# Routing decided from a centered image, product order on GpSimd, and a later routing step in a four-layer MetaFormer kernel

## The chip, the cores and the metric

The kernel runs on one core of a Trainium2 chip, as one launch. The core has five engines that run their own instruction streams in order and wait for each other by semaphores: TensorE (PE; PEld is its weight load), VectorE (DVE), ScalarE (ACT), GpSimd (POOL) and SyncE (SP, which here only issues DMAs). The metric is device microseconds of one execution. The kernel before took 395.4 us, the median of three runs (394.69, 395.40 and 400.83).

## The reference

Four layers act on x of 4 images with 128 channels and 16 x 16 pixels. Each layer adds a convolution-like block to x and then a mixture of experts (MoE), both behind a layer norm over the channels:

```python
x = x + _L0_conv_ref(_ln_c(x), ...)
t = _to_tokens(x)
t = t + _L0_ffn_ref(_ln_t(t), L0_ffn_gate_w, L0_ffn_experts)
...
x = x + _L3_conv_ref(_ln_c(x), L3_conv_conv_w, L3_conv_scale, L3_conv_wf)
t = t + _L3_ffn_ref(_ln_t(t), ...)
```

Layer 0's MoE routes by Sinkhorn and by a choice per expert and image:

```python
gates = jnp.einsum('bhnd,hde->bhne', x4, gate_w)
cg = sinkhorn(gf)                       # clip at 1e-10, 8 times: normalise over tokens, then over experts
vals, idx = jax.lax.top_k(jnp.transpose(cg, (0, 2, 1)), m)   # m = 32 tokens of each expert
gate_values = (vals > 0.5)
outputs = jnp.einsum('hmei,eio->hmeo', routed, experts) * gate_values
s = zeros.at[idx].add(outputs); c = zeros.at[idx].add(1.0)
out = s / (c + 1.0)
```

Layer 3's convolution block is a saliency map: `fm = relu(sal * w)`, `fm = where(fm > TH, fm, 0)`, `1 - wf * sigmoid(scale * fm)`. The MoEs of layers 1 to 3 take each token's two best of 8 experts; that of layer 3 has a hidden width of 256 where the others have 512.

## The kernel before

Channels lie on the 128 partitions and the 1024 pixels (4 images of 256; 8 tiles of 128 tokens) along the free axis. One block of code per engine holds that engine's instructions in program order, and named semaphores (`s["..."]`) order them; there is no scheduler, so the order written is the order run. `step` on DVE issues an instruction and waits for its end before the next one.

Layer 0 ends with an output convolution, image by image. Image 3 is last: DVE adds it to x, PE centers it (`late_center`, into PSUM bank 7), ACT squares it, PE forms the variance of its 256 pixels on all partitions (`late_variance`, L582), ACT takes Ln and Exp (L994, L996), DVE multiplies (L1332), PE forms the gates of tiles 6 and 7 (`gate_tiles`, L586), and DVE clips all gates into `plan`. `keep_clock` issues matmuls on zeros ("quiet", L463) that compute nothing. Then come eight Sinkhorn rounds: PE sums `plan` over tokens (L632) and computes two of the sixteen expert products (`expert_rows`, L625 to L627) while DVE runs six small steps; ACT copies each product out of PSUM (L1043).

After the rounds DVE forms `gate` (plan > 0.5) and `share` = gate / max(1, number of gates of the token) (L1356 to L1359). Tokens' expert outputs are multiplied by their gates: tiles 0 to 4 by ACT (40 ACTIVATEs, L1049) and summed by PE (L650, L651), tiles 5 to 7 by GpSimd (L384) which also sums them (L387, L389). Meanwhile DVE finds each expert's 32 best tokens per row in four rounds of MAX and MATCH_REPLACE (L1364, L1365); PE turns the result (L647), and DVE makes from it a factor per token (`picks`: L1372 to L1378) that scales the sums (L1381 to L1385).

Layers 1 to 3 run six MoE blocks, two halves of x in each layer: 48 units of one expert on 512 columns (block kb = 0 to 5, unit n = 8 kb + j). PE interleaves `front(n+1, f)` (first product) with `back(n, f)` (second product), as `first_half` and `second_half`; each product is three matmuls L440, L441, L442. ACT evaluates each hidden chunk twice (`hidden`, L1082 and L1083), DVE forms the low part (`low`, L1449) that `back` waits for, and `scale` (L1459) weighs a unit's result with its scores; GpSimd adds it to x (`add_part`, L408). While block 4 runs on the one half of x, block 5's half goes through layer 3's convolution block, its norm and its routing: `threshold` (L1588), `saliency_half` (L1593), `center(7, 1)` (L447), `variance(7, 1)` (L452), `logits(5)` (L749), `route_start`, `route_pick` (L1490 to L1502), `route_exp(5)` on ACT (L1088), `route_end` (L1525 to L1533), `turn_route(5)` on PE (L760), `keep_rows(5)` (L1546); SP then writes the scores' rows out and reads them back spread over all partitions (L299, L308). Where each of these stands among the units is written out as (j, f) in the loops.

Of the kernel before, what the change touches and what calls it, by code (L numbers as in the profile page):

```python
# [20 lines left out]
C = 128  # L21
# [42 lines left out]
for _name, _cols in [("center", C), ("mean", C), ("eps6", 1), ("eps5", 1), ("ident", C), ("ones", C),  # L64
# [32 lines left out]
    "gates_done", "expert_out", "expert_kept", "sink_in", "sink_sum", "plan_turned", "plan_ready",  # L97
    "gate_ready", "gated", "gated_sum", "pool_gated", "pool_sum",
# [12 lines left out]
def metaformer(nc, dram, out):  # L111
    ctx = ExitStack()
    with ctx:
# [40 lines left out]
        picked = bot[0:E, :]  # L154

# [35 lines left out]
        pick_w, cnt = piece(64), piece(8)  # L191
# [4 lines left out]
        half_wf, rest_wf, half_b, half_scale = [piece(1) for _ in range(4)]  # L196
        gate, share = oh1, oh2
# [151 lines left out]
        def _(pool):  # L349
# [31 lines left out]
            pool.wait_ge(s["gate_ready"], 1)  # L381
            for t in range(POOL_T, TT):
                tile = wb[:, t, :].rearrange("p (e c) -> p e c", c=C)
                pool.tensor_tensor(tile, tile, over(gate[:, t * E:(t + 1) * E], C), ALU.mult).then_inc(s["pool_gated"], 1)  # L384
# [53 lines left out]
        def _(pe):  # L438
# [141 lines left out]
            def late_variance():  # L580
                pe.wait_ge(s["squared"], 4)
                pe.matmul(bank(0, cols=PIX), k("mean"), image(sq, 3), start=True, stop=True).then_inc(s["variance"], 1)  # L582
# [6 lines left out]
            def early_gates():  # L589
                pe.wait_ge(s["early_normed"], 1)  # L590
                gate_tiles((4, 5))
# [11 lines left out]
            keep_clock(2, 5)  # L603
            late_variance()
            keep_clock(5, 5)
            pe.wait_ge(s["normed"], 4)
            gate_tiles((6, 7)).then_inc(s["gates_done"], 1)
# [325 lines left out]
            for j in range(E):  # L933
# [4 lines left out]
                elif j == 4:  # L938
                    variance(7, 1)
                elif j == 5:  # L940
                    logits(5)
                elif j == 7:
                    turn_route(5)
# [3 lines left out]
                elif j == 2:  # L947
                    saliency(1)
                elif j == 3:
                    center(7, 1)  # L950

# [7 lines left out]
        def _(act):  # L959
# [15 lines left out]
            def norm(n, split=None):  # L975
# [3 lines left out]
                if n == 1:  # L979
# [12 lines left out]
                    act.activation(image(sq, 3), bank(7, cols=PIX), ACT.Square).then_inc(s["squared"], 1)  # L992
                    act.wait_ge(s["variance"], 4)
                    act.activation(image(rstd, 3), bank(0, cols=PIX), ACT.Ln, bias=k("eps5")).then_inc(s["log_var"], 1)  # L994
# [190 lines left out]
            for j in range(0, E + 1):  # L1185
                for f in range(2):
# [18 lines left out]
                    elif (j, f) == (6, 1):  # L1205
# [7 lines left out]
        def _(dve):  # L1213
            steps = [0]

            def step(ins):

                steps[0] += 1
# [112 lines left out]
            dve.wait_ge(s["rstd"], 4)  # L1331
            dve.tensor_tensor(image(xn, 3), bank(7, cols=PIX), image(rstd, 3), ALU.mult).then_inc(s["normed"], 1)  # L1332

            dve.wait_ge(s["gates_done"], 1)
            dve.tensor_scalar(plan, bank(4, cols=64), 1e-10, None, ALU.max).then_inc(s["sink_in"], 1)
            plan3 = tiles(plan)
            for it in range(8):
# [8 lines left out]
                if it == 0:  # L1348
                    dve.wait_ge(s["norm_hi"], 4)
# [9 lines left out]
            step(dve.tensor_tensor(tiles(share), tiles(gate), over(r8b, E), ALU.mult))  # L1359
# [12 lines left out]
            step(dve.tensor_scalar(pick_w, bank(4, cols=64, first=64), 0.0, None, ALU.is_lt))  # L1372
            step(dve.tensor_reduce(cnt, tiles(pick_w), AX.X, ALU.add))
            step(dve.tensor_tensor(pick_w, pick_w, share, ALU.mult))
            step(dve.tensor_scalar(cnt, cnt, 1.0, None, ALU.add))
            step(dve.tensor_reduce(r8, tiles(pick_w), AX.X, ALU.add))
# [348 lines left out]
            for j in range(1, E + 1):  # L1725
                n = 4 * E + j
                for f in range(2):
# [21 lines left out]
                    elif (j, f) == (7, 0):  # L1749
                        route_end(5)  # L1750
                    elif (j, f) == (8, 0):
# [132 lines left out]
```

## Time and profile before

| | before |
|---|---|
| three runs | 394.69, 395.40, 400.83 us |
| the profiled execution | 396.52 us, with a span of 394.5 us from first to last instruction |
| busy: PE, ACT, DVE, POOL | 377.2, 289.7, 260.5, 156.0 us |
| mean granted clock of PE | 0.996 of full speed |
| up to Sinkhorn's first sum (L632) | 52.59 us |
| from there to the factor per token (L1381) | to 83.91 us |
| block 4 with the preparation of block 5 | about 323 to 369 us |

All times are from the start of the span of one profiled execution. A busy PE is not a PE at its peak, since matmuls overlap; what an engine waited for stands in brackets behind the instruction.

### The profile page before, as it was taken

The numbers are of one execution on the slowest core, as the hardware profiler recorded it, in microseconds if no ns is written. First come the engines' busy times: TensorE is split into PE (matmuls) and PEld (weight loads), VectorE is DVE, ScalarE is ACT, GpSimd is POOL, SyncE is SP. The second block draws the span as 40 slices with busy tenths as digits, with TensorE's granted clock in tenths as the row PEclk, the third lists the DMA queues.
The fourth block names the chain that finished last, engine by engine and source line by source line (L and its number), as shares of the span: only waits on it lengthen the run. The fifth ranks groups of instructions, "written<-read, shape, count | busy, mean of one in ns | idle before, by whom it ended". The sixth has DMA issues, their size and how long they took to land.

```text
span 394.5 us, 5148 instructions
## 1 busy us (share of the span) xinstructions
PE 377.2 (96%) x1664; PEld 274.8 (70%) x1668; DVE 260.5 (66%) x570; ACT 289.7 (73%) x515; POOL 156.0 (40%) x135
## 2 busy tenths in 40 slices
PE   8999989989999999999999999999999999989895
PEld 3688856445567687887877677877777777646784
DVE  0755656965434864785675986649957497676776
ACT  4552445935106778978889889999899998867883
POOL 5413000920298265123575781212133356332235
PEclk9999999999999999999999999999999999989999
DMA  7950000000000136604110031151120012220332
GB/s 252 446 197 1 2 0 0 2 0 0 2 0 0 32 135 212 265 2 133 28 53 0 2 109 28 45 200 49 41 95 28 27 27 82 55 80 1 90 99 82
DMA packets 11019, 28.64 MB, mean 73 GB/s; under 512 B 1246, under 2 KB 2526, under 8 KB 10736
## 3 DMA queue, kind: packets, MB, share of 16 engines
q1 hardware_dynamic: 10992, 28.31, 20.7%
q8 instruction: 13, 0.21, 0.2%
q14 instruction: 14, 0.11, 0.1%
HBM read 27.69 MB, written 0.62 MB: 72 GB/s over the span
## 4 chain that ended last, share of the span: by engine, by line
PE 67%; DVE 14%; ACT 14%; issue 3%; POOLq 0%; POOL 0%; DVEq 0%; ACTq 0%
PE ps L440 17%; PE ps L441 16%; PE ps L442 16%; ACT hidh L1082 4%; ACT ps L1083 4%; PE ps L447 4%; DVE hidl L1449 2%; PE ps L738 2%; PE ps L452 2%; ACT rstd L967 1%; DVE bot L1365 1%; ACT rstd L969 1%; PE ps L463 1%; DVE small L1364 1%; PE ps L541 1%
## 5 line engine op out<-in xcount | busy, mean ns | idle before, releaser
L1449 DVE TENSOR_TENSOR hidl<-ps,hidh 128x512 fp32r<-128x512 f32 x160 | 108.4, 687 | 53.7 <-ACT ps L1083 52.3
L408 POOL TENSOR_TENSOR x<-x,parts 128x512 f32<-128x512 f32 x43 | 55.9, 1301 | 149.2 <-DVE parts L1459 98.2
L440 PE MATMUL ps<-xh,wh_all 128*128 128x512 f32 x160 | 74.8, 468 | 2.2 <-DVE hidl L1449 1.7
L1082 ACT ACTIVATE hidh<-ps,par 128x512 fp32r<-128x512 f32 x96 | 68.1, 709 | 9.3 <-PE ps L442 7.6
L440 PE MATMUL ps<-hidh,wh_all 128*128 128x512 f32 (+1 forms) x162 | 64.5, 398 | 4.1 <-DVE hidl L1449 3.8
L1083 ACT ACTIVATE ps<-ps,par 128x512 f32<-128x512 f32 x96 | 65.4, 681 | 0.0
L441 PE MATMUL ps<-xh,wl_all 128*128 128x512 f32 x160 | 63.6, 397 | 0.0
L441 PE MATMUL ps<-hidh,wl_all 128*128 128x512 f32 (+1 forms) x162 | 63.6, 392 | 0.0
L442 PE MATMUL ps<-xl,wh_all 128*128 128x512 f32 x160 | 63.2, 395 | 0.0
L442 PE MATMUL ps<-hidl,wh_all 128*128 128x512 f32 (+1 forms) x162 | 63.1, 390 | 0.0
L398 POOL TENSOR_TENSOR wl_all<-wa,wh_all 128x512 fp32r<-128x512 f32 x40 | 51.3, 1299 | 3.5
L1082 ACT ACTIVATE hidh<-ps 128x512 fp32r<-128x512 f32 x64 | 38.3, 599 | 10.9 <-PE ps L442 10.8
L440 PEld LDWEIGHTS ps<-xh,wh_all 128*128 128x128 f32 x160 | 30.2, 189 | 18.5 <-DVE hidl L1449 7.7
L440 PEld LDWEIGHTS ps<-hidh,wh_all 128*128 128x128 f32 x162 | 30.5, 188 | 14.7 <-DVE hidl L1449 4.8
L1083 ACT ACTIVATE ps<-ps 128x512 f32<-128x512 f32 x64 | 38.4, 600 | 0.0
L441 PEld LDWEIGHTS ps<-xh,wl_all 128*128 128x128 f32 x160 | 30.3, 189 | 9.3 <-issue 4.6
L442 PEld LDWEIGHTS ps<-hidl,wh_all 128*128 128x128 f32 x162 | 30.5, 189 | 7.0
L441 PEld LDWEIGHTS ps<-hidh,wl_all 128*128 128x128 f32 x162 | 30.7, 189 | 6.6
L442 PEld LDWEIGHTS ps<-xl,wh_all 128*128 128x128 f32 x160 | 30.2, 189 | 7.2
L962 ACT ACTIVATE sq<-ps 128x512 f32<-128x512 f32 x15 | 9.2, 610 | 24.0 <-PE ps L447 24.0
L1236 DVE TENSOR_TENSOR xn<-ps,rstd 128x512 f32<-128x512 f32 x13 | 9.0, 692 | 25.3 <-ACT rstd L969 25.3
L1459 DVE SCALAR_TENSOR_TENSOR parts<-ps,par,scores_all 128x512 f32<-128x512 f32 x31 | 23.1, 745 | 2.1 <-PE ps L442 1.8
(254 smaller groups left out, 581.4 us busy)
## 6 DMA issues: line engine op xcount, KB each, us to landing
scores_all<-rows_scratch SPq DMA_DIRECT2D x48, 256.0 KB, 3.4
wa<-in_moe SPq DMA_DIRECT2D x2, 4096.0 KB, 15.6
wa<-in_moe SPq DMA_DIRECT2D x1, 2048.0 KB, 9.2
dft_o<-in_dft_o SPq DMA_DIRECT2D x1, 640.0 KB
w<-in_w_out SPq DMA_DIRECT2D x1, 576.0 KB, 7.8
cst<-in_consts SPq DMA_DIRECT2D x1, 512.5 KB, 6.8
x<-in_x SPq DMA_DIRECT2D x2, 256.0 KB, 3.1
we<-in_w_experts SPq DMA_DIRECT2D x1, 512.0 KB, 8.6
```

Of the source, the lines that this page charges most:

```text
L398: last = pool.tensor_tensor(wl_all[:, e, cols], wa[:, e, cols], f32(wh_all[:, e, cols]), ALU.subtract)
L408: pool.tensor_tensor(half(x, h), half(x, h), parts[:, n % 2, :], ALU.add).then_inc(s["state_added"], 1)
L440: pe.matmul(o, wh, xhi, start=start, stop=False)
L441: pe.matmul(o, wl, xhi, start=False, stop=False)
L442: return pe.matmul(o, wh, xlo, start=False, stop=stop)
L447: pe.matmul(bank(center_bank(n, h)), k("center"), half(x, h), start=True, stop=True).then_inc(s["centered"], 1)
L962: act.activation(work(sq, n, h), bank(center_bank(n, h)), ACT.Square).then_inc(s["squared"], 1)
L1082: act.activation(hidh[:, n % 2, f, :], sums, func, bias=bias).then_inc(s["hidden_hi_act"], 1)
L1083: act.activation(sums, sums, func, bias=bias).then_inc(s["hidden"], 1)
L1236: dve.tensor_tensor(half(xn, h), centered, work(rstd, n, h), ALU.mult).then_inc(s["normed"], 1)
L1449: dve.tensor_tensor(hidl[:, n % 2, f, :], bank(sums_bank(n, f)), f32(hidh[:, n % 2, f, :]), ALU.subtract).then_inc(s["hidden_lo"], 1)
L1459: dve.scalar_tensor_tensor(parts[:, n % 2, :], bank(part_bank(n)), p(spec["b2"])[:, e:e + 1], scores_all[:, slot, :], ALU.add, ALU.mult).t ...
```

## The change

Five edits.

- **Gates of the last image.** DVE copies the centered image out of PSUM (`late`, in the storage of `bot`). PE forms the gates of tiles 6 and 7 from that copy (`late_gates`, bank 3) and the variance of each token as one column per tile (`token_variance`, bank 2); ACT takes Ln and Exp of these two columns; DVE multiplies the gates by them while it clips them into `plan`. The clipping of the other six tiles stands ahead of that. The image's full variance, its Ln and Exp stay, behind this; its normed values are formed after the first round's steps and their low part after the second's. Three quiet matmuls stand where five stood.
- **GpSimd's products** wait for `share` too, and `share` is no longer a `step`.
- **Picks** take six steps where seven stood: the comparison with its 1/8 per expert (in place of the 1.0 that was added later), the comparison times `share` as one instruction, two sums, a reciprocal, a product.
- **`threshold`** compares the values in PSUM bank 7 in place of those in SBUF.
- **Block 5's routing** stands later: `logits(5)` and `turn_route(5)` behind their unit's second half, `route_exp(5)` behind (7, 1) in place of (6, 1), `route_end(5)` behind (7, 1) in place of (7, 0), `keep_rows(5)` behind (8, 1) in place of (8, 0).

```diff
@@ gpsimd
             pool.wait_ge(s["gate_ready"], 1)
+            pool.wait_ge(s["share_ready"], 1)
             for t in range(POOL_T, TT):
...
@@ tensor
             def late_variance():
-                pe.wait_ge(s["squared"], 4)
-                pe.matmul(bank(0, cols=PIX), k("mean"), image(sq, 3), start=True, stop=True).then_inc(s["variance"], 1)
+                pe.wait_ge(s["late_log"], 1)
+                pe.matmul(bank(2, cols=PIX), k("mean"), image(sq, 3), start=True, stop=True).then_inc(s["variance"], 1)
...
-                gate_tiles((4, 5))
+                gate_tiles((4, 5)).then_inc(s["most_gates"], 1)
+
+            def token_variance():
+                pe.wait_ge(s["squared"], 4)
+                for i in range(2):
+                    last = pe.matmul(bank(2, cols=1, first=i), sq[:, (6 + i) * C:(7 + i) * C], k("mean")[:, 0:1], start=True, stop=True)
+                last.then_inc(s["late_variance"], 1)
+
+            def late_gates():
+                pe.wait_ge(s["late_kept"], 1)
+                for i in range(2):
+                    last = pe.matmul(bank(3, cols=E, first=i * E), late[:, i * C:(i + 1) * C], p("gate_w"), start=True, stop=True)
+                last.then_inc(s["gates_done"], 1)
...
             keep_clock(2, 5)
+            token_variance()
+            late_gates()
             late_variance()
-            keep_clock(5, 5)
-            pe.wait_ge(s["normed"], 4)
-            gate_tiles((6, 7)).then_inc(s["gates_done"], 1)
+            keep_clock(3, 5)
...
-                elif j == 5:
-                    logits(5)
-                elif j == 7:
-                    turn_route(5)
                 second_half(4 * E + j)
...
+                elif j == 5:
+                    logits(5)
+                elif j == 7:
+                    turn_route(5)
@@ scalar
+                    act.wait_ge(s["late_variance"], 1)
+                    act.activation(late_rstd, bank(2, cols=2), ACT.Ln, bias=k("eps5")).then_inc(s["late_log"], 1)
+                    act.wait_ge(s["late_log"], 1)
+                    act.activation(late_rstd, late_rstd, ACT.Exp, scale=-0.5).then_inc(s["late_rstd"], 1)
                     act.wait_ge(s["variance"], 4)
...
-                    elif (j, f) == (6, 1):
+                    elif (j, f) == (7, 1):
                         route_exp(5)
@@ vector
-            dve.wait_ge(s["rstd"], 4)
-            dve.tensor_tensor(image(xn, 3), bank(7, cols=PIX), image(rstd, 3), ALU.mult).then_inc(s["normed"], 1)
+            dve.wait_ge(s["centered"], 4)
+            dve.wait_ge(s["squared"], 4)
+            dve.tensor_copy(late, bank(7, cols=PIX)).then_inc(s["late_kept"], 1)
+            dve.wait_ge(s["most_gates"], 1)
+            dve.tensor_scalar(plan[:, 0:6 * E], bank(4, cols=6 * E), 1e-10, None, ALU.max)
             dve.wait_ge(s["gates_done"], 1)
-            dve.tensor_scalar(plan, bank(4, cols=64), 1e-10, None, ALU.max).then_inc(s["sink_in"], 1)
+            dve.wait_ge(s["late_rstd"], 1)
+            for i in range(2):
+                last = dve.tensor_scalar(plan[:, (6 + i) * E:(7 + i) * E], bank(3, cols=E, first=i * E), late_rstd[:, i:i + 1], 1e-10,
+                                         ALU.mult, ALU.max)
+            last.then_inc(s["sink_in"], 1)
...
                 if it == 0:
+                    dve.wait_ge(s["rstd"], 4)
+                    dve.tensor_tensor(image(xn, 3), late, image(rstd, 3), ALU.mult).then_inc(s["normed"], 1)
+                elif it == 1:
...
-            step(dve.tensor_tensor(tiles(share), tiles(gate), over(r8b, E), ALU.mult))
+            dve.tensor_tensor(tiles(share), tiles(gate), over(r8b, E), ALU.mult).then_inc(s["share_ready"], 1)
...
-                dve.scalar_tensor_tensor(fm, fm, TH, fm, ALU.is_gt, ALU.mult).then_inc(s["sal_ready"], 1)
+                dve.scalar_tensor_tensor(fm, bank(7), TH, fm, ALU.is_gt, ALU.mult).then_inc(s["sal_ready"], 1)
```

PE between the last image's centering and the first Sinkhorn sum; `bot` holds the copy of the centered image, `par` the gate weights, `quiet` zeros. Before:

```order
166 L578 MATMUL ps<-x,cst 128x256 [waits x1_ready]
167 L586 MATMUL ps<-par,xn 128x8 [waits early_normed]
168 L586 MATMUL ps<-par,xn 128x8
169 L463 MATMUL ps<-quiet 128x512 x2
170 L582 MATMUL ps<-sq,cst 128x256 [waits squared]
171 L463 MATMUL ps<-quiet 128x512 x5
172 L586 MATMUL ps<-par,xn 128x8 [waits normed]
173 L586 MATMUL ps<-par,xn 128x8
174 L632 MATMUL ps<-small,cst 128x64 [waits we_split,sink_in,norm_lo,norm_hi]
```

Now:

```order
169 L466 MATMUL ps<-quiet 128x512 x2
170 L599 MATMUL ps<-cst,sq 128x1 [waits squared]
171 L599 MATMUL ps<-cst,sq 128x1
172 L605 MATMUL ps<-par,bot 128x8 [waits late_kept]
173 L605 MATMUL ps<-par,bot 128x8
174 L585 MATMUL ps<-sq,cst 128x256 [waits late_log]
175 L466 MATMUL ps<-quiet 128x512 x3
176 L647 MATMUL ps<-small,cst 128x64 [waits we_split,sink_in,norm_lo,norm_hi]
```

The gates no longer wait for `normed`; the full variance and three quiet matmuls now stand between them and the first sum.

DVE around block 5's routing, from the unit before it (`hidl` is `low`, `parts` is `scale`). Before:

```order
412 L1502 MATCH_REPLACE small<-small 128x8 [waits dve_step]
413 L1502 MATCH_REPLACE small<-small 128x8 x3
414 L1449 TENSOR_TENSOR hidl<-ps,hidh 128x512 [waits hidden,hidden_hi_act,dve_step]
415 L1525 SCALAR_TENSOR_TENSOR small<-small 128x32 [waits exp_out]
416 L1526 TENSOR_REDUCE small<-small 128x4 [waits dve_step]
417 L1532 RECIPROCAL small<-small 128x4 [waits dve_step]
418 L1533 TENSOR_TENSOR small<-small 128x32 [waits dve_step]
419 L1459 SCALAR_TENSOR_TENSOR parts<-ps,par,scores_all 128x512 [waits state_added,scores2_in,part_sums]
420 L1449 TENSOR_TENSOR hidl<-ps,hidh 128x512 [waits hidden,hidden_hi_act] x2
421 L1546 COPY rows<-ps 8x512 [waits rows_stored,route_turned]
422 L1459 SCALAR_TENSOR_TENSOR parts<-ps,par,scores_all 128x512 [waits state_added,scores3_in,part_sums]
```

Now:

```order
416 L1476 TENSOR_TENSOR hidl<-ps,hidh 128x512 [waits hidden,hidden_hi_act,dve_step]
417 L1486 SCALAR_TENSOR_TENSOR parts<-ps,par,scores_all 128x512 [waits state_added,scores2_in,part_sums]
418 L1476 TENSOR_TENSOR hidl<-ps,hidh 128x512 [waits hidden,hidden_hi_act]
419 L1552 SCALAR_TENSOR_TENSOR small<-small 128x32 [waits exp_out]
420 L1553 TENSOR_REDUCE small<-small 128x4 [waits dve_step]
421 L1559 RECIPROCAL small<-small 128x4 [waits dve_step]
422 L1560 TENSOR_TENSOR small<-small 128x32 [waits dve_step]
423 L1476 TENSOR_TENSOR hidl<-ps,hidh 128x512 [waits hidden,hidden_hi_act]
424 L1486 SCALAR_TENSOR_TENSOR parts<-ps,par,scores_all 128x512 [waits state_added,scores3_in,part_sums]
425 L1476 TENSOR_TENSOR hidl<-ps,hidh 128x512 [waits hidden,hidden_hi_act]
426 L1573 COPY rows<-ps 8x512 [waits rows_stored,route_turned]
```

The four steps of `route_end` moved from ahead of a unit's scaling to behind it, and the rows leave DVE one chunk later.

The picks on DVE. Before:

```order
111 L1372 TENSOR_SCALAR small<-ps 128x64 [waits picked_turned]
112 L1373 TENSOR_REDUCE small<-small 128x8 [waits dve_step]
113 L1374 TENSOR_TENSOR small<-small 128x64 [waits dve_step]
114 L1375 TENSOR_SCALAR small<-small 128x8 [waits dve_step]
115 L1376 TENSOR_REDUCE small<-small 128x8 [waits dve_step]
116 L1377 RECIPROCAL small<-small 128x8 [waits dve_step]
117 L1378 TENSOR_TENSOR small<-small 128x8 [waits dve_step]
```

Now:

```order
114 L1399 TENSOR_SCALAR small<-ps 128x64 [waits picked_turned]
115 L1401 SCALAR_TENSOR_TENSOR small<-ps,small 128x64 [waits share_ready]
116 L1402 TENSOR_REDUCE small<-small 128x8 [waits dve_step]
117 L1403 TENSOR_REDUCE small<-small 128x8
118 L1404 RECIPROCAL small<-small 128x8 [waits dve_step]
119 L1405 TENSOR_TENSOR small<-small 128x8 [waits dve_step]
```

One instruction fewer, and two that no longer wait for the one ahead of them.

## Rows read from the trace of the kernel before

**Rows 1.** The page: PE's granted clock in 40 slices (tenths).

```profile
PEclk9999999999999999999999999999999999989999
```

**Rows 2.** Chain of waits, last image to Sinkhorn: start us, us, engine and line.

```profile
48.87 0.34 PE ps L586 x4
...
49.66 0.45 PE ps L582 x2
...
51.56 0.63 PE ps L586 x4
...
52.59 0.42 PE ps L632 x2
...
54.57 0.45 PE ps L632 x2
```

**Rows 3.** Timeline: a small Ln on ACT, and quiet matmuls (idle before in brackets).

```profile
104.61 0.27 ACT L1069 ACTIVATE small<-ps,cst 128x4 f32<-128x4 f32 x1 [1.40 <-PE ps L707]
...
49.93 1.24 PE L463 MATMUL ps<-quiet 128*128 128x512 bf16 x5
```

**Rows 4.** Timeline from the shares to the factor per token.

```profile
69.20 11.80 ACT L1049 ACTIVATE wb<-wb,small 128x128 f32<-128x128 f32 x40
69.25 5.61 POOL L384 TENSOR_TENSOR wb<-wb,small 128x1024 f32<-128x1024 f32 x3 [35.38 <-ACT wb L1043]
...
69.58 1.65 DVE L1359 TENSOR_TENSOR small<-small 128x64 f32<-128x64 f32 x1
...
79.59 1.12 PE L650 MATMUL ps<-wb,cst 128*128 128x512 f32 x2
...
80.33 0.99 POOL L389 TENSOR_TENSOR sq<-wb 128x384 f32<-128x384 f32 x1
...
80.56 0.38 PE L651 MATMUL ps<-wb,cst 128*128 128x128 f32 x2
...
81.53 0.65 PE L647 MATMUL ps<-cst,bot 8*128 8x8 f32 x8 [0.59 <-DVE bot L1365]
...
83.91 0.69 DVE L1381 TENSOR_TENSOR sq<-ps,small 128x512 f32<-128x512 f32 x1
```

**Rows 5.** Timeline around layer 3's second threshold (L1588), in block 4.

```profile
344.81 1.28 POOL L408 TENSOR_TENSOR x<-x,parts 128x512 f32<-128x512 f32 x1 [5.58 <-DVE parts L1459]
...
345.27 0.69 DVE L1449 TENSOR_TENSOR hidl<-ps,hidh 128x512 fp32r<-128x512 f32 x1 [0.61 <-ACT ps L1083]
...
346.77 1.38 POOL L408 TENSOR_TENSOR x<-x,parts 128x512 f32<-128x512 f32 x1 [0.68 <-DVE parts L1459]
...
346.93 1.77 DVE L1588 SCALAR_TENSOR_TENSOR sq<-sq 128x512 f32<-128x512 f32 x1
...
349.36 0.50 PE L440 MATMUL ps<-hidh,wh_all 128*128 128x512 f32 x1 [1.61 <-DVE hidl L1449]
...
352.16 0.60 ACT L962 ACTIVATE sq<-ps 128x512 f32<-128x512 f32 x1 [0.42 <-PE ps L447]
...
353.50 0.69 ACT L1082 ACTIVATE hidh<-ps,par 128x512 fp32r<-128x512 f32 x1 [0.74 <-PE ps L442]
```

**Rows 6.** Busy time in a stretch: length, PE, PEld, DVE, ACT, POOL, clock, DMA, GB/s.

```profile
350.00:354.00 4.00, 4.00 (x9) 2.28 (x8) 2.19 (x4) 2.84 (x6) 1.27 (x1) 0.57 0.13 44
```

**Rows 7.** Timeline: block 4's routing (first row), then block 5's.

```profile
321.16 0.98 DVE L1525 SCALAR_TENSOR_TENSOR small<-small 128x32 f32<-128x32 f32 x1
...
363.62 0.23 ACT L1088 ACTIVATE small<-small 128x32 f32<-128x32 f32 x1 [2.27 <-DVE small L1494]
...
365.95 0.47 PE L440 MATMUL ps<-hidh,wh_all 128*128 128x512 f32 x1 [1.37 <-DVE hidl L1449]
...
370.50 14.62 SPq L308 DMA_DIRECT2D scores_all<-rows_scratch  x8
...
375.71 0.74 DVE L1459 SCALAR_TENSOR_TENSOR parts<-ps,par,scores_all 128x512 f32<-128x512 f32 x1
```

**Rows 8.** The page: DMA issues, with size and median us to landing.

```profile
scores_all<-rows_scratch SPq DMA_DIRECT2D x48, 256.0 KB, 3.4
```

More of the change, by code:

```diff
@@ L96 @@
     "out_conv_done", "x1_ready",
-    "gates_done", "expert_out", "expert_kept", "sink_in", "sink_sum", "plan_turned", "plan_ready",
-    "gate_ready", "gated", "gated_sum", "pool_gated", "pool_sum",
+    "most_gates", "gates_done", "late_kept", "late_variance", "late_log", "late_rstd", "expert_out", "expert_kept", "sink_in", "sink_sum", "plan_turned", "plan_ready",
+    "gate_ready", "share_ready", "gated", "gated_sum", "pool_gated", "pool_sum",
     "picked", "picked_turned", "combined", "combined_turned", "x2_ready",
@@ L154, in metaformer @@
         picked = bot[0:E, :]
+        late = bot[:, 0:PIX]
         with ExitStack() as scope:
@@ L190, in metaformer @@
         plan, r8, r8b, top8 = piece(64), piece(8), piece(8), piece(8, E)
-        pick_w, cnt = piece(64), piece(8)
+        pick_w, pick_s, cnt = piece(64), piece(64), piece(8)
         kmx, kbias, kes, krs = [piece(4, KK) for _ in range(4)]
@@ L196, in metaformer @@
         half_wf, rest_wf, half_b, half_scale = [piece(1) for _ in range(4)]
+        late_rstd = piece(2)
         gate, share = oh1, oh2
@@ L992, in norm @@
                     act.activation(image(sq, 3), bank(7, cols=PIX), ACT.Square).then_inc(s["squared"], 1)
+                    act.wait_ge(s["late_variance"], 1)
+                    act.activation(late_rstd, bank(2, cols=2), ACT.Ln, bias=k("eps5")).then_inc(s["late_log"], 1)
+                    act.wait_ge(s["late_log"], 1)
+                    act.activation(late_rstd, late_rstd, ACT.Exp, scale=-0.5).then_inc(s["late_rstd"], 1)
                     act.wait_ge(s["variance"], 4)
-                    act.activation(image(rstd, 3), bank(0, cols=PIX), ACT.Ln, bias=k("eps5")).then_inc(s["log_var"], 1)
+                    act.activation(image(rstd, 3), bank(2, cols=PIX), ACT.Ln, bias=k("eps5")).then_inc(s["log_var"], 1)
                     act.wait_ge(s["log_var"], 4)
@@ L1214, in _, with step @@
             steps = [0]
-            def step(ins):
-                steps[0] += 1
+            def step(ins, n=1):
+                steps[0] += n
                 ins.then_inc(s["dve_step"], 1)
@@ L1370, in _ @@
             dve.wait_ge(s["picked_turned"], 1)
[L1372 to L1376, printed above, removed]
+            marks = bank(4, cols=64, first=64)
+            dve.tensor_scalar(pick_w, marks, 0.0, 1.0 / E, ALU.is_lt, ALU.add).then_inc(s["dve_step"], 1)
+            dve.wait_ge(s["share_ready"], 1)
+            step(dve.scalar_tensor_tensor(pick_s, marks, 0.0, share, ALU.is_lt, ALU.mult), 2)
+            dve.tensor_reduce(cnt, tiles(pick_w), AX.X, ALU.add).then_inc(s["dve_step"], 1)
+            step(dve.tensor_reduce(r8, tiles(pick_s), AX.X, ALU.add), 2)
             step(dve.reciprocal(r8b, cnt))
@@ L1748, in _ @@
                         route_pick(5)
-                    elif (j, f) == (7, 0):
+                    elif (j, f) == (7, 1):
                         route_end(5)
-                    elif (j, f) == (8, 0):
+                    elif (j, f) == (8, 1):
                         keep_rows(5)
```

## The prediction

> **What bounds the kernel now.** I read the page first. PE is busy for nearly all of the span (the table above), and its granted clock is at full speed in all slices but one, the thirty-sixth [rows 1]. So most of the span is PE's own work, which the change leaves as it is; it can win only where PE waits for a decision, or runs at the lower clock. Three such places touch the edits.
>
> The first, in the chain of waits, is the last image's way to Sinkhorn: everything from its variance at 49.66 to the first sum at 52.59 hangs on one chain over PE, ACT, DVE and PE again [rows 2]. The rounds behind it repeat at 52.59, 54.57 and so on, 2.0 us each, and DVE's small steps and the sum set their pace, so whatever moves the first sum moves all of them.
>
> The second is the stretch from the shares to the factor per token [rows 4]. The last share instruction on DVE, a product of 128x64, shows 1.65 us, where seven later steps of that size take 1.73 together (82.18, L647's end, to 83.91). GpSimd's first product runs from 69.25 for 1.87 (5.61 for three), to 71.12; the share ends at 71.23. It stood behind GpSimd.
>
> The third is the second threshold in block 4: 1.77 us, while GpSimd's addition runs from 346.77 to 348.15 [rows 5]. PE then waits 1.61 us for the low part behind it, and from 350 to 354 the granted clock averages 0.57 [rows 6]: the lower of the two levels, 1.2 GHz, for most of it. No other slice has such a fall [rows 1]. Later in block 4 ACT waits 2.27 us for the routing and PE 1.37 us [rows 7].
>
> **Gates of the last image.** The old chain is variance, Ln, Exp, product, gates, clipping. The new one is shorter on ACT and DVE, but PE does its work in order, and I follow PE. It is free of quiet matmuls at 49.66. The token variances are four passes like those of L586, 0.34; the gates four more, 0.34. Then, still ahead of the first sum, come the full variance, 0.45 as before [rows 2], and three quiet matmuls, three fifths of 1.24 = 0.74 [rows 3]. The sum can start at 49.66 + 0.34 + 0.34 + 0.45 + 0.74 = 51.53. Is `plan` there by then? Ln of two columns is nearest to the 0.27 of four [rows 3]; with as much for Exp and twice 0.25 for the clipping it is ready at 50.0 + 0.27 + 0.27 + 0.5 = 51.0. So PE's queue ends last, and the gain is 52.59 - 51.53 = 1.06; I take **1.0**. Bounds: 0.5, if each group of four passes costs the 0.63 that L586 shows behind an idle PE [rows 2], to 1.5, if the variance and the quiet matmuls cost nothing. The copy of the centered image on DVE runs beside the token variances. The moved product and low part fall into the first and second round's wait for the sum on PE (0.45 each [rows 2]); if that cover failed, each would cost what it overruns. ACT copies expert products one round later, and has the rest of the rounds to catch up.
>
> **Shares and picks.** With GpSimd behind the shares, L1359 takes about 0.25: DVE's search starts 1.4 us sooner, and ends near 80.1 in place of 81.5. GpSimd starts some 0.65 later and ends at 81.32 + 0.65 = 81.97 [rows 4]; its sums are wanted behind L1381, so that is covered. But the 1.4 us do not all arrive. When the search ends, PE still has the seventh expert's pair to finish, until 80.94, so the turning starts there and ends at about 81.6. From there the steps took 1.73; one step fewer, and two that don't wait, leave about 1.3: 82.95. PE's last pair, behind the turning, takes 1.35 (79.59 to 80.94) and ends near 82.9 as well. ACT's forty products end at 81.0 either way. So L1381 starts near 83.0 and not at 83.91: **0.9**. Bounds: 0.4, if a step with two operands in SBUF meets GpSimd's last addition; 1.5, where ACT's end at 81.0 and PE's last 1.35 alone decide.
>
> **Threshold.** The low part L1449 at 345.27 reads one operand in PSUM and one in SBUF, and takes 0.69 though GpSimd's addition covers nearly all of it (344.81 to 346.09) [rows 5]. The threshold's new form reads the same way, so I price it at 0.74, as the scaled product L1459 of that form [rows 7]: 1.03 less. PE's wait of 1.61 then shrinks to 0.6. A wait of 1.37 us at 364.6 was followed by no fall of the clock [rows 1, 7], so I expect none here; at an average of 0.57 PE lost 4 x 0.43 = 1.7 us of work [rows 6]. PE would be 1.03 + 1.7 = 2.7 us ahead at the next variance. ACT can't follow all the way: besides the 1.03 it had only 0.42 and 0.74 of waiting for PE to give up there [rows 5], so what reaches the norm and the routing of block 5 is 1.03 + 0.42 + 0.74 = **2.2**. Bounds: 1.0, if the clock falls all the same; 2.7, if ACT is not the limit.
>
> The Trainium skill (SBUF — State Buffer, section "SBUF: two separate sides") states that DVE, with two SBUF inputs, and GpSimd take a shared pair of ports for a whole instruction, and that the later one blocks. The ends 71.23 behind 71.12 and 348.70 behind 348.15 agree with that [rows 4, 5]. By this rule the next edit loses on DVE; if DVE and GpSimd shared the ports without blocking, the sum would be 4.8 us in place of 4.1.
>
> **Block 5's routing later.** ACT no longer waits 2.27 us, and PE's wait for the low part behind the routing's picks shortens by the hidden chunk that ACT evaluates earlier, about half of 1.37: 0.7 won. But the moved end of the routing now comes behind a unit's scaling, which starts GpSimd's addition of some 1.3 us [rows 5]. In block 4's routing the same instruction, L1525, stands like that, and takes 0.98 [rows 7]. PE, which turns the result, waits that much longer: some 0.7 lost. I take **0**, with 0.7 either way. The rows leave DVE a chunk later in the program. Before, the reads of the scores were issued from 370.50, and the first one was used at 375.71 [rows 7], 5.2 us later; against the 3.4 that the page gives for landing [rows 8], that is 1.8 of slack. The units come 2.2 earlier and the rows only about 0.4, so the slack is just used up.
>
> **The sum.** 1.0 + 0.9 + 2.2 + 0 = 4.1 us. All three lie ahead of PE-bound work that follows at its own pace, so they should stay in the span: 394.5 becomes 390.4, and the profiled execution's 396.5 becomes 392.4. Its time stands 1.1 above the median of the runs, 395.4; on that scale the forecast is **391.3**.
>
> **Rivals.**
> - *The clock still falls in block 4*, there or at one of the shorter waits left behind it. For: the page shows that PE is one long wait from it. Against: a wait of 1.37 passed unharmed. Then the threshold is worth only 1.0, the sum 2.9: 392.5.
> - *The late rows starve the last block.* DVE would wait for the scores at its first scaling, with the low parts that PE needs queued behind it. For: the slack is used up, by the count above. Against: the low parts are a chunk ahead of PE there. With 1 to 2 us of waiting it costs as much at most: 392.3 to 393.3.
> - *Slower: the clock falls at Sinkhorn's start.* Two quiet matmuls are gone just where PE waits. At half speed a round is bound by PE: a sum of 0.45 [rows 2] and six product matmuls, which fill most of the round's 2.0 now, would take some 3.5, 1.5 more per round. Three slow rounds eat the gain; all eight cost 12, and the time would be 403. Against: in the new order PE has work from 49.66 to the sum with hardly a gap, and in the old order it stood idle behind its five quiet matmuls and kept the clock.
> - *No collision*, so that the late routing wins its 0.7 and the picks come at their bound: 5.4 in all, 390.0.
>
> **How the numbers follow.** The forecast gets 64 in 100, the clock in block 4 13, the late rows 9, the slower case 4, the better case 10. The terms' own bounds, not all at one end, reach from 2.0 to 5.8: 389.6 to 393.4. Some of the first two rivals' share, with the spread of about 1 us between runs that this kernel shows (394.69, 395.40), takes the upper end to 394.2. A change of 2%, about what a measurement of this kernel can tell from no change, is 7.9 us: faster by that needs nearly twice the sum, 0.04; slower by that needs nearly all eight rounds at half speed, 0.03; within it, 0.93.
>
> **What would show it.** The first Sinkhorn sum about 1.0 earlier, right behind the quiet matmuls; the last share at 0.25 and GpSimd's first product behind it; L1381 1.9 earlier by the clock of the span; both thresholds near 0.74, and no clock below full speed in any slice; ACT's 2.27 gone, and L1525's successor at about 1 us behind a scaling. I am wrong if the first sum waits for `plan`, or if PE's waits in block 4 come back elsewhere so that the last block starts less than 3 us earlier.

## The result, and the profile after

| | before | after |
|---|---|---|
| median, 22 runs each | 395.65 us | 393.94 us |
| the 22 runs | 394.45 to 400.85 | 392.16 to 397.08 |
| profiled execution | 396.52, span 394.5 | 392.55, span 390.6 |

The ratio, formed from fast runs alone (a run is slow when it lies over 1.5% above the fastest of its kernel), is 0.9949 [0.9929, 0.9969]: the change gained about 2 us by it and 1.7 by the medians, where 4.1 were forecast. The profiled execution alone did what was forecast, 396.52 to 392.55 against 392.4. So two things have to be explained: which terms of the sum are right in that execution, and why the median moved by less than half as much.

For after and for all later runs, the span and PE's mean granted clock of each run are on record. They are used to sort the runs, because the clock turned out to be the difference between them.

The page of after, with its span and the clock in 40 slices, stands against [rows 1]; the slice at 350 us is at full speed now:

```profile
span 390.6 us, 5157 instructions
...
PEclk9999999999999999999999999999999999999999
```

**A common point.** Two spans can't be laid over each other from their start. Up to 49 us both kernels run the same work, yet the low part of the third image on DVE, ahead of every edit, starts at different times. It is the first row of each fence; the second is DVE's reading of the first Sinkhorn sum. Timeline rows of before:

```profile
48.88 0.43 DVE L1330 TENSOR_TENSOR xl<-xn,xh 128x256 fp32r<-128x256 f32 x1 [0.48 <-ACT xh L990]
...
53.03 0.23 DVE L1342 TENSOR_REDUCE small<-ps 128x8 f32<-128x64 f32 x1 [0.59 <-PE ps L632]
```

and of after:

```profile
49.18 0.43 DVE L1349 TENSOR_TENSOR xl<-xn,xh 128x256 fp32r<-128x256 f32 x1 [0.48 <-ACT xh L1005]
...
52.20 0.23 DVE L1365 TENSOR_REDUCE small<-ps 128x8 f32<-128x64 f32 x1 [0.90 <-PE ps L647]
```

After comes 0.30 later here, and not by an edit: over the fourteen traces of this study this row lies between 47.77 and 49.18, in no order of the edits, and at 48.88 and 48.52 in two executions of the kernel before. From this row to the sum, before takes 4.15 us and after 3.02: the gates gained **1.13**. Read from the start of the span it would be 0.83. Every "shift" below is counted from this row.

PE's way to that sum in after, from the chain of waits (start us, us, engine and line); compare [rows 2]:

```profile
50.30 0.48 PE ps L605 x4
50.78 0.57 PE ps L585 x2
51.35 0.65 PE ps L466 x3
```

It is the order that the prediction followed: gates, full variance, three quiet matmuls, sum, with no wait for `plan`. (The chain leaves out the token variances, L599, which come ahead of these.)

The stretch from the shares to the factor per token in after (timeline); compare [rows 4]:

```profile
68.36 11.81 ACT L1068 ACTIVATE wb<-wb,small 128x128 f32<-128x128 f32 x40
...
68.75 0.23 DVE L1385 TENSOR_TENSOR small<-small 128x64 f32<-128x64 f32 x1
...
69.14 5.62 POOL L387 TENSOR_TENSOR wb<-wb,small 128x1024 f32<-128x1024 f32 x3 [34.99 <-DVE small L1385]
...
80.04 0.66 PE L662 MATMUL ps<-cst,bot 8*128 8x8 f32 x8
...
81.59 0.38 PE L666 MATMUL ps<-wb,cst 128*128 128x128 f32 x2
...
82.08 0.69 DVE L1408 TENSOR_TENSOR sq<-ps,small 128x512 f32<-128x512 f32 x1 [0.16 <-PE ps L666]
```

The share takes 0.23 in place of 1.65, and GpSimd starts behind it. The turning (L662) starts when PE ends the seventh pair, and what L1408 waits for last, by 0.16 us, is PE's last pair (L666): the bound that the prediction named. It starts at 82.08 against 83.91, a shift of -2.13, of which the gates are 1.13.

The threshold in block 4 in after, with PE's wait behind it, and block 5's routing (timeline); compare [rows 5, 7]:

```profile
345.02 1.40 POOL L411 TENSOR_TENSOR x<-x,parts 128x512 f32<-128x512 f32 x1 [0.68 <-DVE parts L1486]
...
345.19 0.68 DVE L1615 SCALAR_TENSOR_TENSOR sq<-ps,sq 128x512 f32<-128x512 f32 x1
...
346.52 0.50 PE L443 MATMUL ps<-hidh,wh_all 128*128 128x512 f32 x1 [0.52 <-DVE hidl L1476]
...
355.26 0.50 PE L443 MATMUL ps<-hidh,wh_all 128*128 128x512 f32 x1 [0.93 <-DVE hidl L1476]
...
361.11 0.47 PE L443 MATMUL ps<-hidh,wh_all 128*128 128x512 f32 x1 [0.52 <-DVE hidl L1476]
...
362.13 0.97 DVE L1552 SCALAR_TENSOR_TENSOR small<-small 128x32 f32<-128x32 f32 x1
...
363.82 0.60 PE L775 MATMUL ps<-cst,small 128*8 128x128 f32 x4 [0.39 <-DVE small L1560]
```

The threshold takes 0.68, within GpSimd's addition from its start to its end, and PE's wait of 1.61 is 0.52. The one wait of 1.37 is gone, and three stand in its stead: 0.93, 0.52 and 0.39. From the common point to the end of the span the shift is -4.19.

### The profile page after: what moved, and what is told of

It is laid out like the page before. It is cut to its first block, busy times and chain, and to the rows that moved or that the text cites. A ratio compares the mean times of both kernels' runs of the same rounds, so it can differ in the third digit from the quotient of the medians.

```text
span 390.6 us, 5157 instructions
## 1 busy us (share of the span) xinstructions
PE 375.9 (96%) x1666; PEld 274.5 (70%) x1670; DVE 259.5 (66%) x572; ACT 290.1 (74%) x517; POOL 156.0 (40%) x135
## 4 chain that ended last, share of the span: by engine, by line
PE 69%; ACT 17%; DVE 10%; issue 3%; POOLq 0%; POOL 0%; DVEq 0%
PE ps L443 17%; PE ps L444 16%; PE ps L445 16%; ACT hidh L1101 4%; ACT ps L1102 4%; PE ps L450 3%; ACT wb L1068 3%; PE ps L753 2%; PE ps L455 2%; DVE hidl L1476 2%; PE ps L466 1%; ACT rstd L982 1%; ACT rstd L984 1%; PE ps L544 1%; PE ps L647 1%
```

## The experiments

**The two kernels once more.** No edit.

> The kernel before, unchanged, for the granted clock of each of its runs. Theory (edits worth what was forecast, clock falls decide the median): several groups of runs by mean granted clock; the group at 0.996, that of the profiled execution with its one fall at 350 us, near 394.5 us of span, and the groups at lower clocks some us longer. Rival (the shortfall lies in the edits, and the runs' clocks say nothing): one clock for all runs, and spans that don't follow it.

> The changed kernel, unchanged, for its groups by clock and for the trace of another execution. Theory: groups at 0.998, 0.989 and 0.983 with spans near 390.4, 392.1 and 395.1 again; should the trace be of a run at 0.989, it shows a stretch of some 8 us at the lower level, with about 1.7 us lost, and all else as in the first trace. Rival (edits that wobble by themselves): a trace at 0.989 has the clock's fall in the tail only, and the 1.7 us go somewhere else.

Before again: 395.40 (12 runs), ratio 1.0006 [0.9971, 1.0042]. After again: 394.64 (12 runs), ratio 0.9957 [0.9927, 0.9987]. The gain of about 2 us is real, and it is not the profiled execution's 4. The trace of after_again shows why. Busy time in stretches (length, then busy us and count of PE, PEld, DVE, ACT, POOL; granted clock; DMA share, GB/s):

```profile
92.00:97.00 5.00, 4.73 (x40) 4.49 (x39) 2.78 (x9) 2.63 (x10) 0.00 (x0) 1.00 0.00 0
97.00:98.00 1.00, 1.00 (x3) 0.36 (x2) 0.45 (x1) 0.00 (x0) 0.00 (x0) 0.70 0.06 16
98.00:104.00 6.00, 6.00 (x22) 4.72 (x21) 1.24 (x4) 0.60 (x1) 0.00 (x0) 0.50 0.00 0
104.00:105.00 1.00, 1.00 (x5) 0.29 (x3) 0.89 (x3) 0.00 (x0) 0.00 (x0) 0.89 0.00 0
```

and the same in the first profiled execution of after:

```profile
92.00:97.00 5.00, 4.74 (x41) 4.49 (x41) 2.91 (x8) 2.88 (x10) 0.00 (x0) 1.00 0.00 0
97.00:98.00 1.00, 1.00 (x5) 0.50 (x4) 0.57 (x1) 0.00 (x0) 0.00 (x0) 1.00 0.06 16
98.00:104.00 6.00, 5.72 (x29) 3.34 (x27) 2.73 (x10) 1.32 (x4) 0.00 (x0) 1.00 0.00 0
```

At 97 us, after the same work, the clock falls in one execution to the lower level (1.2 of 2.4 GHz) for about 7 us, and not in the other. The shift is -2.13 ahead of it in both; behind it -2.13 in the one, +0.47 in the other: the fall cost **2.6 us**. What PE did before it, in after_again's timeline:

```profile
92.57 1.95 PE L699 MATMUL ps<-par,xn 128*128 128x128 f32 x16
94.79 1.98 PE L705 MATMUL ps<-key_d,keye 49*128 49x49 f32 x16 [0.27 <-DVE key_d L1431]
96.70 1.43 PE L691 MATMUL ps<-img_t,dft_x 128*128 128x512 f32 x2
97.92 3.49 PE L716 MATMUL ps<-key_t,img_w 128*128 128x49 f32 x16
```

PE counts as busy for 4.73 of the 5 us ahead, but with narrow matmuls: 16 of 128 columns, then 16 of 49. This is the preparation of the keys' filter, which no edit touches. Only one execution of each experiment has a trace; for the other runs the mean clock has to tell which had a fall. Traces with the fall at 97 show 0.987 to 0.991, those with the one at 350 alone 0.996, those with neither 0.997 to 1.0 (with a lower clock in some of the last microseconds, when PE has no more work). So sorted, with the median span (before: the runs with a clock on record, which leaves out the 22 above):

| mean clock | under 0.992 | 0.992 to 0.9964 | from 0.9965 |
|---|---|---|---|
| before, 102 runs | 19 at 397.8 | 35 at 394.6 | 48 at 392.95 |
| after, 34 runs | 22 at 392.5 | none | 12 at 390.45 |

By this sorting the fall at 97 sits in after's median run and in few of before's; the one at 350 [rows 6] sat in the profiled execution of before, but 48 of its 102 runs have neither. No trace shows a run at 0.983, of which after has four, nor one at 0.980 to 0.986, which 17 of before's 19 show; their spans are longer still, and they may hold more than one fall. All runs below are sorted by the same bounds.

**The threshold alone, and the routing undone.** Before, with the one line of the threshold:

```diff
-                dve.scalar_tensor_tensor(fm, fm, TH, fm, ALU.is_gt, ALU.mult).then_inc(s["sal_ready"], 1)
+                dve.scalar_tensor_tensor(fm, bank(7), TH, fm, ALU.is_gt, ALU.mult).then_inc(s["sal_ready"], 1)
```

> The kernel before with the threshold's operand in PSUM alone. Theory: L1588 at 0.7 us, PE's wait behind it at 0.6 to 0.7, no fall of the clock at 350 us, the span 2.2 us shorter than before at a like clock (392.3). Rival (the clock falls there all the same): only 1.0 shorter, 393.5, with the clock near 0.996.

394.37 (12 runs), ratio 0.9969 [0.9940, 0.9999]; ten of the runs have spans of 392.0 to 392.7, none a clock between 0.992 and 0.9964: the fall at 350 is gone, in the trace and, by the mean clock, in these ten runs. Timeline, then a stretch as above:

```profile
346.88 0.68 DVE L1588 SCALAR_TENSOR_TENSOR sq<-ps,sq 128x512 f32<-128x512 f32 x1
...
348.22 0.50 PE L440 MATMUL ps<-hidh,wh_all 128*128 128x512 f32 x1 [0.52 <-DVE hidl L1449]
...
350.00:354.00 4.00, 4.00 (x16) 2.83 (x15) 2.22 (x5) 3.97 (x7) 1.28 (x1) 1.00 0.19 66
```

The shift goes from +0.26 ahead of the threshold to -2.04 behind it: 2.3 against the profiled execution of before, with its fall; without the fall only about half (below).

After, with block 5's routing where it was:

```diff
-                elif j == 5:
-                    logits(5)
-                elif j == 7:
-                    turn_route(5)
                 second_half(4 * E + j)
...
-                    elif (j, f) == (7, 1):
+                    elif (j, f) == (6, 1):
                         route_exp(5)
```

(with the logits and the turning ahead of `second_half` again, and `route_end` and `keep_rows` at their old places)

> The changed kernel with block 5's routing where it was. Theory (the late routing is worth 0): 390.4 without a fall, within 0.3 of the changed kernel. Rivals: 391.1 if the late routing wins its 0.7, 389.7 if it loses 0.7. The groups at 0.989 and 0.983 as often as in the changed kernel, 22 in 34, since all of it comes behind 97 us.

394.18 (12 runs), ratio 0.9949 [0.9919, 0.9979]: as after's. The old waits are back (timeline):

```profile
355.42 1.06 PE L764 MATMUL ps<-par,xn 128*128 128x8 f32 x8 [0.43 <-DVE xn L1255]
...
360.87 0.23 ACT L1107 ACTIVATE small<-small 128x32 f32<-128x32 f32 x1 [2.26 <-DVE small L1521]
...
362.97 0.18 DVE L1552 SCALAR_TENSOR_TENSOR small<-small 128x32 f32<-128x32 f32 x1
...
363.20 0.47 PE L443 MATMUL ps<-hidh,wh_all 128*128 128x512 f32 x1 [1.38 <-DVE hidl L1476]
```

From 345 us to the end the shift grows by 1.81 here and by 2.12 in after, so the later routing is worth about 0.3 us, which the medians don't show. PE's waits there add up to 1.84 in after and, with one of 0.43 for the logits, to 1.81 here: they were moved, not removed. In after L1552 costs 0.97 in place of 0.18, as foreseen.

**The gates alone and the picks alone.** Before, with only the edits of the last image's gates (on PE as below, with their parts on ACT and DVE); and before, with only `share_ready` and the picks in six steps:

```diff
             keep_clock(2, 5)
+            token_variance()
+            late_gates()
             late_variance()
-            keep_clock(5, 5)
-            pe.wait_ge(s["normed"], 4)
-            gate_tiles((6, 7)).then_inc(s["gates_done"], 1)
+            keep_clock(3, 5)
```

```diff
+            pool.wait_ge(s["share_ready"], 1)
...
-            step(dve.tensor_tensor(tiles(share), tiles(gate), over(r8b, E), ALU.mult))
+            dve.tensor_tensor(tiles(share), tiles(gate), over(r8b, E), ALU.mult).then_inc(s["share_ready"], 1)
```

> The kernel before with the gates of the last image from its centered state, and nothing else of the change. Theory: the first Sinkhorn sum about 0.8 to 1.0 earlier, and spans 1.0 shorter than before at a like clock: about 392.0 without a fall of the clock, 393.5 with the one at 350 us. If what decides the fall at 97 us is when that stage comes, its share of runs (clock 0.98 to 0.99) differs from the 8 in 47 of before, in either direction. Rival (the fall at 97 us comes from the two quiet matmuls left out): about two runs in three, as in the changed kernel.

> The kernel before with GpSimd behind the shares and the picks in six steps, and nothing else. Theory: the last share at 0.25, L1381's successor 0.9 earlier, spans 0.9 shorter at a like clock: about 392.1 without a fall, 393.6 with the one at 350 us. By the rival that the fall at 97 us comes from the missing quiet matmuls: no more of it than before, 8 in 47.

By their medians both look worthless: 396.91, ratio 1.0018 [0.9984, 1.0052], and 395.98, ratio 1.0035 [1.0000, 1.0070]. By the mean clock, half of the runs with the gates alone have the fall at 97 (six of 12 under 0.992), and five of 12 with the picks alone. The traces tell what the edits do. Shifts in us against the profiled execution of before:

| up to | gates alone | picks alone | threshold alone | after |
|---|---|---|---|---|
| first Sinkhorn sums | -1.13 | 0 | 0 | -1.13 |
| behind the factor per token | -1.13 | -1.00 | 0 | -2.13 |
| 107 us in before | +2.69 | -1.01 | 0 | -2.13 |
| 345 us in before | +2.86 | -0.55 | +0.26 | -2.07 |
| 353 us in before | +1.65 | -0.49 | -2.04 | -4.38 |
| the end | +2.01 | -0.05 | -1.90 | -4.19 |

The first two terms add up exactly, and the threshold's comes on top. The gates alone lost 3.8 us at the same place, which comes at 99 us in that trace (stretches):

```profile
94.00:99.00 5.00, 4.73 (x37) 3.99 (x35) 2.46 (x7) 1.79 (x6) 0.00 (x0) 1.00 0.01 3
99.00:100.00 1.00, 1.00 (x8) 1.00 (x7) 0.00 (x0) 0.00 (x0) 0.00 (x0) 0.57 0.00 0
100.00:105.00 5.00, 5.00 (x16) 3.34 (x15) 1.59 (x5) 0.60 (x1) 0.00 (x0) 0.50 0.00 0
```

That trace also has no fall at 350, though the threshold is the old one there: against the execution of before, which has one, the shift falls from +2.86 to +1.65, and these 1.2 us are what the fall at 350 costs. The picks alone give 0.4 back between 107 and 111 us; after does not, and what it was stays open.

**Two quiet matmuls back at Sinkhorn's start.**

```diff
-            keep_clock(3, 5)
+            keep_clock(5, 5)
```

> The changed kernel with five quiet matmuls behind the full variance, as before, in place of three. If the runs at 0.989 and 0.983 come from a fall of the clock at Sinkhorn's start, for want of the two quiet matmuls: those groups vanish or grow rare, and the span is about 390.4 + 0.5 = 390.9, the two matmuls' own time. If the falls come from elsewhere: the same groups, each 0.5 us longer.

393.38 (12 runs), ratio 0.9929 [0.9894, 0.9963]: the two matmuls cost 0.43 us there (the shift at the first sums is -0.70 in place of -1.13), and yet the median is 1.3 under after_again's in the same comparison, since only three of 12 runs are under 0.992. Three more are at 0.995, with spans 1.5 us over those without a fall; no trace shows where. So leaving two matmuls out costs nothing at Sinkhorn's start, but with them the fall at 97, some 45 us later, is rarer. Whether by the moment at which the keys come or otherwise, this run doesn't tell.

**PE work at the fall itself.** After, with four matmuls on zeros between the two narrow groups, twice, and with two:

```diff
+            keep_clock(4, 2)
             pe.wait_ge(s["key_diag"], 1)
```

> The changed kernel with four quiet matmuls ahead of the turned keys (behind L699, into a bank that is free), where PE waits for DVE between groups of narrow matmuls. If the fall at 97 us follows from how little PE does from 92 to 97 us: no run, or nearly none, at 0.983 to 0.989, and a median within 0.6 of 392.4 in all runs, the four costing 0.3 to 0.6. If it is a matter of when the stage comes alone, or of something earlier: still about two runs in three.

> The changed kernel with four matmuls on zeros between the first filter layer (L699, 16 narrow matmuls) and the turn of the keys (L705, 16 of 49 columns), once more. In the traces, counted from a common point at 45 us, these four cost 0.52 us, and a clock fall at 97 to 105 us costs 2.61 us. Theory A (the fall at 97 us is what the changed kernel's median run lost, and little PE work ahead of it brings it): no run with a mean granted clock at 0.98 to 0.99, spans of 390 to 392 us, a median of 393.0 +-0.5, ratio to before 0.992 to 0.994. Rival (the six runs of the first time were luck, the changed kernel's share of falls being 22 of 34): about eight of twelve runs at 0.98 to 0.99 with spans of 392.5 to 394, a median of 394.5.

> The same with two of the four matmuls on zeros. PE waited 0.27 us for the keys in that place, so two of 0.26 us each cost about 0.25 us less than four: 0 to 0.26 us against the changed kernel without a fall. Theory A: where two are enough, no run at 0.98 to 0.99, and the median is 0.2 to 0.3 us under that of four; where they are not, some of the runs show the fall and spans 2.6 us longer, and the median is between 392.8 and 394.5.

393.03 (6 runs), ratio 0.9924 [0.9896, 0.9951]; 392.76 (9 runs), ratio 0.9908 [0.9875, 0.9942]; with two 392.41 (6 runs), ratio 0.9908 [0.9873, 0.9943]. None of these 21 runs is under 0.992, against 22 of 34 of after; seven are at 0.996, with spans like the others' (389.5 to 391.4, beside 389.9 to 391.2). Four cost 0.52 us by the shift (-1.61 behind them), two 0.09 (-2.04), since PE waited there anyway. In the trace with two:

```profile
92.19 1.95 PE L699 MATMUL ps<-par,xn 128*128 128x128 f32 x16
93.97 0.59 PE L466 MATMUL ps<-quiet 128*128 128x512 bf16 x2
94.50 1.98 PE L706 MATMUL ps<-key_d,keye 49*128 49x49 f32 x16
```

The version with two has the lowest median of the study, 1.5 us under after's of the first comparison; its ratio is 0.9908 against 0.9949 and 0.9957 of after, with intervals that still overlap.

After, with the four matmuls 7 us earlier, behind the last image's variance:

```diff
-            keep_clock(5, 7)
+            keep_clock(9, 7)
```

> The changed kernel with four matmuls on zeros more behind the last image's variance (L679, nine in place of five, at 88 us in its trace), none at 95 us. PE waits 0.23 us for the normalized image there, so they cost 0.8 us or less. If the narrow matmuls from 92 to 97 us alone bring the fall, it stays in half to two thirds of the runs (0.98 to 0.99, spans about 3 us over the others) and the median is 394.5 to 395.3; if matmuls anywhere in that neighbourhood, or another moment of arrival, are enough to prevent it, few runs show it and the median is 393.3 to 393.9.

395.57 (12 runs), ratio 0.9984 [0.9952, 1.0017]; ten of the 12 runs are under 0.992. There they don't keep the clock up. In the trace, first the timeline, then stretches:

```profile
87.07 2.11 PE L466 MATMUL ps<-quiet 128*128 128x512 bf16 x9
...
91.89 2.25 PE L699 MATMUL ps<-par,xn 128*128 128x128 f32 x16
94.48 1.98 PE L705 MATMUL ps<-key_d,keye 49*128 49x49 f32 x16 [0.34 <-DVE key_d L1431]
...
91.00:96.00 5.00, 4.62 (x39) 4.24 (x38) 3.18 (x10) 2.88 (x10) 0.00 (x0) 1.00 0.00 0
...
97.00:106.00 9.00, 9.00 (x27) 6.13 (x26) 2.27 (x7) 0.84 (x2) 0.00 (x0) 0.50 0.00 0
```

So matmuls of full width among the narrow ones, between 92 and 97 us, keep the clock up, and the same matmuls shortly before don't. It is not the only thing that counts: with five quiet matmuls at Sinkhorn's start the fall was rarer too, with the narrow stretch as it was.

**The same four matmuls in the kernel before**, at the same place (L687 there), with the same edit.

> The kernel before with the same four matmuls on zeros ahead of the turn of the keys, and nothing else of the change. Theory A: its runs at 0.98 to 0.987 (8 of 47 without them) vanish, and the other runs get 0.5 us longer: spans of 392.7 to 395.2 us, a median of 395.9 +-0.6, ratio 0.999 to 1.004; so the four matmuls are no gain by themselves, and the gain of the changed kernel with them is the change's own. Rival (the four matmuls gain by themselves, whatever kernel they stand in, so that the change is worth 2 us and they are worth 1 us): a median of 394.6 or less.

395.86 (12 runs), ratio 1.0009 [0.9986, 1.0032]; none of the runs is under 0.992, and the four cost before 0.51 us by the shift. The matmuls are no gain of their own in before; beside them, in the same comparison, the change is worth 395.86 - 392.76 = **3.1 us**. The trace of before_warm settles another point (timeline, then a stretch):

```profile
349.85 0.50 PE L440 MATMUL ps<-hidh,wh_all 128*128 128x512 f32 x1 [1.61 <-DVE hidl L1450]
...
350.00:354.00 4.00, 4.00 (x14) 2.32 (x14) 2.68 (x4) 3.98 (x8) 1.28 (x1) 1.00 0.06 22
```

PE's wait of 1.61 is the same as in [rows 5], and no fall follows. In before_again it does:

```profile
350.00:354.00 4.00, 4.00 (x9) 2.50 (x9) 1.95 (x3) 2.62 (x5) 1.29 (x1) 0.57 0.17 54
```

## Why the prediction was wrong

- **Gates, 1.0:** right; 1.13. PE's queue ended last, as followed, and the clock held at Sinkhorn's start in every trace: the slower rival did not come.
- **Shares and picks, 0.9:** right; 1.00, with PE's last pair as the bound. By the Trainium skill (SBUF — State Buffer, section "SBUF: two separate sides"), a DVE instruction with two SBUF inputs and a GpSimd instruction that reads SBUF hold a shared pair of ports against each other for a whole instruction. The share, 1.65 behind GpSimd's product and 0.23 ahead of it, and the threshold, 1.77 with both operands in SBUF and 0.68 with one in PSUM, agree with it.
- **Threshold, 2.2:** right in that one execution, 2.3; but it is two things. In before_warm and gates_only the old threshold passes without a fall, 1.2 us cheaper. So 1.2 of the 2.3 is the fall at 350, and about 1.1 is the threshold itself, close to the 1.03 that the prediction read from the two durations. Its 1.7 for the clock was too large by itself, but ACT's waits cut it to 0.42 + 0.74 = 1.16, which is what the fall costs; and in the trace with the threshold alone ACT is busy for 3.97 of the 4 us at 350, against 2.84 [rows 6]. What it had wrong is to count this part as won in every run.
- **Routing, 0 with 0.7 either way:** right; about 0.3, the old waits traded for shorter ones of the same sum. The late rows did not starve the last block.
- **The sum, 4.1:** right against the profiled execution, 4.19 from the common point. That it met one of the 12 runs of after without a fall, and not one of the 22 with it, is luck. **The step that failed is the next one**, where the prediction set the profiled execution's gain against the median of the runs ("on that scale the forecast is 391.3"). That takes for granted that the profiled execution's clock is that of the median run, before and after. It was not. In before, the 1.2 us of the fall at 350 can only be won in runs that have it, and 48 of 102 have none; the median of the first 22 runs, 395.65, lies 0.9 below the profiled execution's 396.52. In after, the median run has the fall at 97: its group lies at 392.5, 2 us over the runs without one. About half of the profiled gain is paid out there. Without any fall the two kernels differ by 392.95 - 390.45 = 2.5 us by their groups, and by 3.1 with matmuls that keep the clock up at 97 in both. The terms without the fall at 350 make 1.13 + 1.00 + 1.1 = 3.2, less the 0.1 to 0.4 that the traces give back between 353 us and the end; what gives it back stays open.
- **The rivals:** the clock was looked for at two places that the edits touch. It fell at a third, 15 us behind the second edit, where the code is the same. The prediction argued from one trace that a wait had "passed unharmed". The longer wait of 1.61 passes in one execution and not in another, so one trace is too little to call a wait safe.

**What stays open** is why the changed kernel meets the fall at 97 in 22 of 34 runs and the old one, by the mean clock, in at most 19 of 102. The stretch ahead of it shows the same work in both, only 2.1 us earlier. The share of such runs moves with small shifts ahead of it (two of 12 with the threshold alone, six with the gates alone, three with five quiet matmuls, ten with four more at 88 us), in no order that the shifts explain by themselves.

The traces hold one thing that goes with it. The clock first reaches full speed at 4.1 to 7.1 us, at another moment in each execution, and the work follows that only in part. PE's first four matmuls on x, in after, after_again and routing_undone, whose code is the same up to 97 us (timeline):

```profile
4.28 3.32 PE L450 MATMUL ps<-x,cst 128*128 128x512 f32 x4
4.28 2.36 PE L450 MATMUL ps<-x,cst 128*128 128x512 f32 x4
4.21 1.88 PE L450 MATMUL ps<-x,cst 128*128 128x512 f32 x4
```

By the traces' clock records the rise comes at 7.06, 5.24 and 4.14 us, and the turn of the keys (L705 in after) starts 88.0, 89.6 and 89.5 us behind it; the first execution has no fall at 97, the other two have it. Over the ten traces without matmuls on zeros at the keys, the turn starts 89.0 to 90.0 us behind the rise in the four with the fall, and 88.0 or 90.5 to 91.2 us behind it in the six without. PE's wait of 1.6 behind the old threshold ends 343.5 to 343.8 us behind the rise in the three traces with the fall at 350, and 344.6 and 345.5 in the two without. So where the work stands against the clock's own rise sorts these traces; no experiment moved that on purpose, so it is not shown to be the cause.

The Trainium skill (TensorE: Matmul & The Clock Gate, section "What's actually happening") says that the window in which activity is judged runs freely and does not start with the kernel. That the same code falls in one execution and not in the next agrees with it, but no run here shows the window. That before's own runs under 0.992 are falls at 97 was not seen in a trace; their absence in before_warm (0 of 12) fits, with few runs.

## What to carry to other kernels

Sort the timed runs by span and mean granted clock before a profiled execution is set against their median; a term that rests on a clock fall is worth, on the mean, its price times the share of the runs that have it. When an edit brings a stretch of narrow matmuls to another moment, look at the clock there, even where no edit touches the code, and try a matmul or two of full width among them where PE waits anyway; here that kept the clock up in 21 of 21 runs. Compare traces from a common instruction ahead of the first edit: here the start alone moved the whole by up to 1.4 us, more than either of the first two terms.

## What the hardware did that was not expected

- The same program takes the fall or not from run to run: at 97 us in 22 of 34 runs of after by their mean clock. In the four traces that have it, of after and three relatives, it lasts 7 to 10 us at a granted clock of 0.50 and costs 2.6 to 3.8 us (2 us between the medians of after's two groups).
- PE counted as busy for 4.73 of the 5 us ahead of the fall in after_again. Two matmuls of 512 columns among the narrow ones, 0.09 us longer, went with no fall in 6 of 6 runs; four of them 7 us earlier with a fall in 10 of 12.
- Medians alone would have rejected two edits that gain 1.13 and 1.00 us by their traces, since each on its own came, by the mean clock, with more falls than before has.
